# Mixing the last layer's result with the old state by one VectorE instruction instead of a diagonal matmul

## The chip, the core and the metric

One core of a Trainium2 chip runs the whole program once. The metric is the device time of that one execution in microseconds (us); the number given for a kernel is the median of several runs.

## What is computed

A graph with 6,250 nodes of 256 features and 100,000 edges passes two layers. The last part of the second layer is the one that matters here. For each node the messages of six relations have been summed; they are averaged, multiplied by a weight matrix of the node's type, mixed with the old state, normalized over the 256 features, and added to the residual:

```python
present = cnt.reshape(n, r) > 0
nrel = jnp.maximum(present.sum(-1), 1).astype(x.dtype)
t = (t_rel * present[..., None].astype(x.dtype)).sum(1) / nrel[:, None]
trans = typed_linear(t, Wa, ba)
alpha = jax.nn.sigmoid(skip)[node_type][:, None]
out = trans * alpha + x * (1.0 - alpha)
mu = out.mean(-1, keepdims=True)
var = out.var(-1, keepdims=True)
normed = (out - mu) * jax.lax.rsqrt(var + LN_EPS) * ln_g[node_type] + ln_b[node_type]
has_msg = present.any(-1)[:, None]
return jnp.where(has_msg, normed, x)          # the caller adds this to its own x
```

## The kernel before, in words

The program is a row of stages; the last one, `nodes_out`, works on 51 batches of 128 nodes, all nodes of a batch having one type. It is a software pipeline written out by hand. Each engine runs its own list of small functions, and `run_stages` gives each function a lag: in step s an engine runs, in the order of its list, the function with lag L for batch s - L. The loop body is unrolled four times, and semaphores join the engines.

The way of one batch: SyncE loads the node numbers (`load_in`). GpSimd gathers the relation sums of the 128 nodes from memory (`gather`, L1932, tile `acc_in`, lag 0). VectorE counts the relations that have messages (`counts`, L2044, lag 1), makes one factor for each relation and head (`at_least_one`, `masses`, `inverses`), and multiplies the whole gathered tile by them (`means`, L2074, 128 x 1536 elements, lag 1). TensorE transposes this (`turn`, L2160, lag 2) and ScalarE copies it out of PSUM (`mean_out`). TensorE multiplies by the relations' matrices (`relate`, L2170, lag 3), ScalarE copies again (`sum_out`), and TensorE runs `project` (lag 4). That one sums into `trans_p` in PSUM: two recorded matmuls with `keep_diag`, a diagonal matrix that holds 1 - alpha, and the old state `h1` (L2182); one matmul for the bias (L2184); four recorded ones for the weights, which hold alpha already (L2188). ScalarE makes `keep_diag` anew for each batch (`keep_part`, L1972). VectorE takes the statistics of `trans_p` (`stats` L2107, `variance` L2115, lag 4), ScalarE the root, VectorE the reciprocal and the shift (`scale` L2122, `shifts` L2127, lag 5), and ScalarE normalizes `trans_p` into `normed` (`norm`, L1998, lag 5). GpSimd multiplies by the type's gamma and adds its beta (`affine`, L1942 and L1947, lag 6). VectorE adds the rest (`finish`, L2139, tile `res`, lag 7; `other` was made by `others`, L2092, lag 3), and GpSimd scatters the batch to the output (`scatter`, L1957, lag 7).

Three orders matter. GpSimd's step is gather, scatter, affine. TensorE's is turn, project, relate. VectorE's is

```python
((1, counts), (7, finish), (1, at_least_one), (5, scale), (1, masses), (5, shifts), (1, inverses),
 (3, is_absent), (1, means), (4, stats), (3, others), (4, is_present), (4, variance))
```

so that `counts` of step s waits for the gather of batch s - 1, and all later functions of the step stand behind it. SyncE's step is load_in, load_x (lag 1), load_out (lag 5).

Of the kernel before, what the change touches and what calls it, by code (L numbers as in the profile page):

```python
# [24 lines left out]
ds = bass.ds  # L25
# [79 lines left out]
def wait_slot(eng, sems, item, dmas=1):  # L105

    eng.wait_ge(sems[item.slot(item.unroll)], item.round() * (16 * dmas))
# [1703 lines left out]
def nodes_out(nc, c):  # L1811
# [5 lines left out]
    with ExitStack() as ctx:  # L1817
        def sb(name, shape, dt=F32):
            return ctx.enter_context(nc.sbuf_tensor(name, shape, dt))
# [11 lines left out]
        x1, h1 = [t[:, 0:D] for t in x1h1], [t[:, D:2 * D] for t in x1h1]  # L1831
        type_f, keep_b = sb("type_of_f", [1, BATCHES]), sb("keep_of_batch", [P, BATCHES])
        of_kind = sb("batch_of_kind", [P, TYPES, BATCHES])
        keep_diag = [sb(f"keep_diag{k}", [P, P]) for k in range(2)]
        b_part = [sb(f"b_a_part{j}", [P, TYPES, D], BF16) for j in range(PARTS)]
        b_rest = sb("b_a_rest", [P, TYPES, D])
        b_rows, one_rows = sb("b_a_rows", [P, TYPES, D], BF16), sb("one_rows", [P, P], BF16)
# [33 lines left out]
        scaled_ready, biased_ready, res_ready = sem("scaled_o"), sem("biased_o"), sem("res_o")  # L1871
        stored, held = sems("out_stored", UN), sem("out_held")
        rows_filled, keep_ready, bias_ready = sem("b_a_rows_zero"), sem("keep_h_ready"), sem("b_a_parts")
        types_spread, kinds_ready, diag_ready = sem("types_spread"), sem("kinds_ready"), sem("keep_diag_ready")
        LANE, ROWS = 32, 96
        READY = 2 + PARTS
        acc_rows = c["acc_d"][0:NP * RELS, :].rearrange("(n r) f -> n (r f)", r=RELS)[0:N, :]
# [14 lines left out]
        with nc.Block() as block:  # L1892
            @block.sync
            def _(sp):
                def load_in(it):
                    k = it.slot(UN)
                    rows = ds(it.index * P, P)
                    rounds(sp, gathered, it)
                    sp.sem_inc(held, 1)
                    sp.dma_start(who_in[k][:], c["who_d"][rows, :]).then_inc(who_in_loaded[k], 16)  # L1900

                def load_x(it):
                    k = it.slot(UN)
                    rows = ds(it.index * P, P)
                    wait(sp, other_ready, it, UN)
                    sp.sem_inc(held, 1)
                    wait(sp, trans_summed, it, UN)
                    sp.sem_inc(held, 1)
                    sp.dma_start(x1h1[k][:], c["x1h1_d"][rows, :]).then_inc(x_loaded[k], 16)

                def load_out(it):
                    k = it.slot(UN)
                    rows = ds(it.index * P, P)
                    rounds(sp, stored, it)
                    sp.sem_inc(held, 1)
                    sp.dma_start(who_out[k][:], c["who_d"][rows, :]).then_inc(who_out_loaded[k], 16)

                run_stages(sp, BATCHES, ((0, load_in), (1, load_x), (5, load_out)), UN)
                for k in range(UN):
                    sp.wait_ge(stored[k], 16 * len(range(k, BATCHES, UN)))  # L1920
# [42 lines left out]
            @block.scalar  # L1963
            def _(act):
                act.activation(gain[:], skip[:], ACT.Sigmoid).then_inc(gain_ready, 1)

                def keep_part(it):
                    k = it.slot(2)
                    if isinstance(it.i, int) and it.index == 0:
                        act.wait_ge(w_ready, READY)  # L1970
                    wait(act, trans_summed, it, 2)
                    act.activation(keep_diag[k][:], c["ident"][:], ACT.Copy,  # L1972
                                   scale=keep_b[:, ds(it.index, 1)]).then_inc(diag_ready, 1)

                def mean_out(it):
                    k = it.slot(2)
                    wait(act, tT_summed, it, 2)
                    for pair in range(PAIRS):
                        act.wait_ge(meanT_turned, it.count(1, PAIRS, pair + 1))
                        act.copy(meanT[k][:, 2 * pair:2 * pair + 2], meanT_p[pair][:]).then_inc(meanT_ready, 1)  # L1980

                def sum_out(it):
                    k = it.slot(2)
                    wait(act, tT_summed, it)
                    wait(act, trans_summed, it, 2)
                    act.copy(tT[k][:], tT_p[:]).then_inc(tT_ready, 1)

                def root(it):
                    k = it.slot(UN)
                    wait(act, var_ready, it)  # L1990
                    wait(act, shift_ready, it, UN)
                    act.activation(std[k][:], mv[k][:, 1:2], ACT.Sqrt, bias=c["eps"][:]).then_inc(std_ready, 1)

                def norm(it):
                    k = it.slot(UN)
                    wait(act, shift_ready, it)
                    wait(act, res_ready, it, UN)
                    act.activation(normed[k][:], trans_p[it.slot(2)][:, 0:D], ACT.Identity, bias=shift[k][:],  # L1998
                                   scale=rstd[k][:]).then_inc(normed_ready, 1)

                run_stages(act, BATCHES, ((2, mean_out), (5, norm), (3, keep_part), (3, sum_out), (4, root)), UN)

            @block.vector
            def _(dve):
# [94 lines left out]
                    wait(dve, res_ready, it, UN)  # L2099
                    dve.tensor_scalar(present[k][:], count[k][:], 0.5, None, ALU.is_gt).then_inc(present_ready, 1)  # L2100

                def stats(it):
                    k = it.slot(UN)
                    wait(dve, trans_summed, it)
                    dve.sem_inc(held, 1)
                    wait(dve, var_ready, it, UN)
                    dve.bn_stats(stat[k][:], trans_p[it.slot(2)][:, 0:D]).then_inc(stat_ready, 1)  # L2107

                def variance(it):
                    k = it.slot(UN)  # L2110
# [19 lines left out]
                def finish(it):  # L2130
# [8 lines left out]
                    dve.scalar_tensor_tensor(res[k][:], normed[k][:], present[k][:], other[k][:], ALU.mult,  # L2139
                                             ALU.add).then_inc(res_ready, 1)  # L2140

                run_stages(dve, BATCHES, ((1, counts), (7, finish), (1, at_least_one), (5, scale), (1, masses),
                                          (5, shifts), (1, inverses), (3, is_absent), (1, means), (4, stats),
                                          (3, others), (4, is_present), (4, variance)), UN)

            @block.tensor
            def _(pe):
                kind = pe.alloc_register("kind_pe")
                pe.wait_ge(rows_filled, 2)
                pe.matmul(trans_p[0][:, 0:BATCHES], ones_f[:], type_f[:], start=True, stop=True).then_inc(types_spread, 1)  # L2150

                def turn(it):
                    k = it.slot(2)
                    wait(pe, mean_ready, it)
                    for pair in range(PAIRS):
                        if not (isinstance(it.i, int) and it.index == 0):
                            pe.wait_ge(meanT_ready, it.count(2, PAIRS, pair + 1))
                        for j in range(2):
                            for a in range(HALF):
                                ins = pe.transpose(meanT_p[pair][:, j, a, :], mean[k][:, 2 * pair + j, a * P:(a + 1) * P],  # L2160
                                                   c["ident"][:])
                        ins.then_inc(meanT_turned, 1)

                def relate(it):
                    k = it.slot(2)
                    wait(pe, meanT_ready, it, per=PAIRS)
                    wait(pe, tT_ready, it, 1)
                    for a in range(HALF):
                        for r in range(RELS):
                            ins = pe.matmul(tT_p[:, a, :], m_rel[:, r, a, :], meanT[k][:, r, a, :],  # L2170
                                            start=r == 0, stop=r == RELS - 1)
                    ins.then_inc(tT_summed, 1)

                def project(it):
                    k = it.slot(2)
                    t = type_of(pe, kind, it)
                    if isinstance(it.i, int) and it.index == 0:
                        pe.wait_ge(w_ready, READY)
                    wait(pe, normed_ready, it, 2)
                    wait_slot(pe, x_loaded, it)  # L2180
                    wait(pe, diag_ready, it)
                    pe.matmul(trans_p[k][:, 0:D], keep_diag[k][:], h1[it.slot(UN)],  # L2182
                              start=True, stop=False)
                    pe.matmul(trans_p[k][:, 0:D], one_rows[0:ROWS, :],  # L2184
                              b_rows[0:ROWS, ds(t, 1), :].rearrange("p o n -> p (o n)"), start=False, stop=False)
                    wait(pe, tT_ready, it)
                    for a in range(HALF):
                        ins = pe.matmul(trans_p[k][:, 0:D], tT[k][:, a, :],  # L2188
                                        w_a[:, ds(t * HALF + a, 1), :].rearrange("p o n -> p (o n)"),
                                        start=False, stop=a == HALF - 1)  # L2190
                    ins.then_inc(trans_summed, 1)

                run_stages(pe, BATCHES, ((2, turn), (4, project), (3, relate)), UN)


# [89 lines left out]
```

## Time and profile before

| | us |
|---|---|
| median of 3 runs | 3666.56 |
| lowest and highest | 3665.77, 3671.32 |
| the profiled execution | 3659.42 |
| its span in the trace | 3657.6 |
| start of `nodes_out` in the trace | 3329.3 |
| TensorE busy over the span | 3381.2 (92%) |
| VectorE busy over the span | 3185.6 (87%) |
| GpSimd busy over the span | 2390.0 (65%) |

The profile is of one execution. The times in its rows are counted from the start of the span. The stage that the change touches is the last 328 us.

### The profile page before, as it was taken

What the parts mean: (1) busy time and instruction counts of PE and PEld (TensorE: products, weight loads), DVE (VectorE), ACT (ScalarE), POOL (GpSimd) and SP (SyncE); (2) the same over time, 40 slices, a digit from 0 to 9 for tenths busy, and PEclk for the clock granted to TensorE, in tenths of its full rate; (3) what the DMA queues carried; (4) which work ended last, traced back from release to release, by engine and by line L of the source; (5) the groups of instructions that cost most, each with busy time, mean ns of one, the idle gap of its engine ahead of it and who ended that gap; (6) DMA issues with size and microseconds to landing.
All of it is one profiled execution on the core that took longest, in us unless ns stands there. A gap on an engine that the chain in (4) does not pass through costs nothing. (4 is left out here: it accounts for less than half of the span.)

```text
span 3657.6 us, 111781 instructions
## 1 busy us (share of the span) xinstructions
PE 3381.2 (92%) x25829; PEld 2771.8 (76%) x25830; DVE 3185.6 (87%) x9898; ACT 2594.7 (71%) x7607; POOL 2390.0 (65%) x2549
## 2 busy tenths in 40 slices
PE   3979999999999997996999999999999999997997
PEld 2547777777777775775888888888888888886996
DVE  6768999999999995664999999999999999996775
ACT  1856777777777774543878888888888888884553
POOL 3756777777777763554666666666666666663775
PEclk8989999999999997998999999999999999998998
DMA  3979999999999984776888888888888888884663
GB/s 102 263 230 309 301 296 301 298 298 298 299 298 300 300 253 165 276 258 224 254 235 239 240 236 239 237 239 237 238 238 239 238 237 239 236 237 150 213 208 126
DMA packets 604966, 898.40 MB, mean 246 GB/s; under 512 B 208971, under 2 KB 418646, under 8 KB 604371
## 3 DMA queue, kind: packets, MB, share of 16 engines
q0 software_dynamic: 164240, 566.71, 50.5%
q1 hardware_dynamic: 440643, 330.78, 30.2%
q8 instruction: 28, 0.46, 0.1%
q14 instruction: 55, 0.45, 0.0%
HBM read 724.25 MB, written 175.28 MB: 246 GB/s over the span
## 5 line engine op out<-in xcount | busy, mean ns | idle before, releaser
L1595 POOL DMA_INDIRECT kv1c<-kv_table,rec x900 | 865.9, 962 | 299.0 <-issue 284.6
L916 POOL DMA_INDIRECT kv<-kv_table,rec x832 | 848.3, 1020 | 282.3 <-issue 258.2
L1700 DVE CUSTOM_DVE_ANT_0 masked_scores<-score_p,far 126x384 f32<-126x384 f32 x1200 | 595.6, 551 | 30.2 <-issue 14.1
L1640 ACT ACTIVATE wv<-kv1c,wv 128x64 f32<-128x64 f32 x2400 | 605.9, 335 | 17.7
L954 ACT ACTIVATE gates<-gates_p 128x512 f32<-128x512 f32 x832 | 448.3, 591 | 77.5 <-PE gates_p L1087 77.5
L1803 PE MATMUL sum_p<-wv,hot 128*126 128x260 f32 x1800 | 477.7, 402 | 1.4 <-ACT wv L1640 1.4
L1759 PE MATMUL qe_p<-qrel,hotT 126*128 126x256 f32 x1800 | 443.0, 382 | 22.7 <-ACT hotT L1625 18.1
L1107 PE MATMUL sum_p<-msg,hot_weighted 128*124 128x256 f32 x1664 | 416.2, 393 | 5.3 <-ACT hot_weighted L962 5.3
L1759 PEld LDWEIGHTS qe_p<-qrel,hotT 126*128 126x128 f32 x1800 | 343.7, 191 | 74.9 <-ACT hotT L1625 18.7
L1107 PEld LDWEIGHTS sum_p<-msg,hot_weighted 128*124 128x124 f32 x1664 | 295.2, 187 | 116.2 <-issue 73.9
L1803 PEld LDWEIGHTS sum_p<-wv,hot 128*126 128x126 f32 x1800 | 316.1, 189 | 76.1 <-ACT wv L1640 1.8
L1605 POOL TENSOR_TENSOR faded<-acc,fade 126x260 f32<-126x260 f32 x300 | 186.2, 621 | 265.2 <-ACT fade L1648 255.2
L1680 DVE TENSOR_TENSOR qk<-qe_p,kv1c 128x768 f32<-128x768 f32 x300 | 285.7, 952 | 79.8 <-issue 47.7
L1783 PE MATMUL score_p<-scoreT,spread_head 32*126 32x128 f32 x7200 | 347.9, 282 | 0.8 <-ACT scoreT L1654 0.8
L1026 DVE CUSTOM_DVE_ANT_0 qe_p<-qe_p,gates 128x256 f32<-128x256 f32 x832 | 326.1, 452 | 0.0
L1792 PEld LDWEIGHTS peak_p<-peak,hotT 126*128 126x128 f32 x1800 | 223.4, 191 | 107.2 <-DVE peak L1708 71.0
L1792 PE MATMUL peak_p<-peak,hotT 126*128 126x4 f32 x1800 | 249.0, 256 | 52.1 <-DVE peak L1708 46.3
L1783 PEld LDWEIGHTS score_p<-scoreT,spread_head 32*126 32x126 f32 x7200 | 290.4, 184 | 6.4 <-ACT scoreT L1654 1.3
L1686 DVE TENSOR_REDUCE score_lanes<-qk 128x12 f32<-128x768 f32 x300 | 285.8, 953 | 4.8
L1011 DVE TENSOR_TENSOR qe_p<-qe_p,kv 128x1024 f32<-128x1024 f32 x208 | 254.8, 1225 | 12.2 <-DMA kv<-kv_table,rec 10.2
L1096 PEld LDWEIGHTS qe_p<-q_blk,hotT 124*128 124x128 f32 x1664 | 210.8, 189 | 71.6 <-issue 63.2
L962 ACT ACTIVATE hot_weighted<-hot,weight 128x124 f32<-128x124 bf16 x832 | 263.1, 388 | 0.2 <-DVE weight L1043 0.2
(285 smaller groups left out, 7392.0 us busy)
## 6 DMA issues: line engine op xcount, KB each, us to landing
key<-segment_keys SPq DMA_DIRECT2D x300, 192.0 KB
q_blk<-q_table SPq DMA_DIRECT2D x208, 256.5 KB
acc_table<-acc SPq DMA_DIRECT2D x300, 130.0 KB
qrel<-q_by_relation SPq DMA_DIRECT2D x300, 128.0 KB
feat<-in_edge_feat_t SPq DMA_DIRECT2D x208, 128.0 KB
agg_and_x_plus_h<-total SPq DMA_DIRECT2D x208, 128.0 KB
kv1c<-kv_table,rec POOLq DMA_INDIRECT x900
kv<-kv_table,rec POOLq DMA_INDIRECT x832
```

What stands on the lines that cost most here:

```text
L916: pool.indirect_dma_start(kv[it.slot(AHEAD)][:, t, :], None, c["kv0_d"], bass.IndirectOffsetOnAxis(ap=rec[k][:, t, 0:1].bitcast(I32), axis ...
L954: act.activation(gates[k][:, t, :], gates_p[t][:], ACT.Silu).then_inc(gates_ready, 1)
L1026: ins = dve.tensor_tensor_reduce(qe_p[:, t, :], qe_p[:, t, :], gates[k][:, t, 0:D], 1.0, 0.0, ALU.mult, ALU.add, attn[k][:, t:t + 1])
L1107: ins = pe.matmul(sum_p[:, k, :], hot_w[k][:, t, :], msg[k][:, t, :], start=t == 0, stop=t == T0 - 1)
L1595: pool.indirect_dma_start(kv[k][:, t, :], None, c["kv1_d"], bass.IndirectOffsetOnAxis(ap=rec[k][:, t, 0:1].bitcast(I32), axis=0)).then_inc ...
L1640: ins = act.activation(wv[k][:, t, h, 0:DK], kv[s][:, t, D + h * DK:D + (h + 1) * DK], ACT.Copy, scale=wv[k][:, t, h, DK:DK + 1])
L1686: dve.tensor_reduce(score[it.slot(U1)], qk[it.slot(2)][:], AX, ALU.add).then_inc(score_ready, 1)
L1700: dve.tensor_tensor_reduce(junk[k][:, h], score_p[:, :, h, :], far[it.slot(U1)][:], 1.0, FLOOR, ALU.subtract, ALU.max, top[s][:, h:h + 1]) ...
L1759: ins = pe.matmul(qe_p[:, t, :], hotT[k][:, t, :], qrel[s][0:SEG], start=True, stop=True)
L1783: ins = pe.matmul(score_p[:, t, h, :], spread_head[rows, h, :], scoreT[k][rows, :], start=True, stop=True)
L1792: ins = pe.matmul(peak_p[:, t, :], hotT[k][:, t, :], peak[it.slot(U1)][:], start=True, stop=True)
L1803: ins = pe.matmul(sum_p[:], hot[s][:, t, :], wv[k][:, t].rearrange("p h e -> p (h e)"), start=t == 0, stop=t == T1 - 1)
```

## The change

ScalarE's `keep_part` and TensorE's two recorded matmuls with `keep_diag` go. A new VectorE function `mix` (lag 4) reads the projection from PSUM, the old state `h1` and the factor of the batch, and writes the mixed state to a new tile `trans` in SBUF (four buffers). `stats` and `norm` read `trans`; TensorE's `project` waits for the `mix` of two batches before, where it waited for `norm`; SyncE's `load_x` waits for `mix`, where it waited for the projection. VectorE's list gets a new order: `others`, `mix` and `stats` now stand ahead of `means`.

```diff
-        keep_diag = [sb(f"keep_diag{k}", [P, P]) for k in range(2)]
+        trans = [sb(f"trans{k}", [P, D]) for k in range(UN)]
...
-                    wait(sp, trans_summed, it, UN)
+                    wait(sp, mixed_ready, it, UN)
...
-                def keep_part(it):
-                    k = it.slot(2)
-                    if isinstance(it.i, int) and it.index == 0:
-                        act.wait_ge(w_ready, READY)
-                    wait(act, trans_summed, it, 2)
-                    act.activation(keep_diag[k][:], c["ident"][:], ACT.Copy,
-                                   scale=keep_b[:, ds(it.index, 1)]).then_inc(diag_ready, 1)
-
...
-                    act.activation(normed[k][:], trans_p[it.slot(2)][:, 0:D], ACT.Identity, bias=shift[k][:],
+                    act.activation(normed[k][:], trans[k][:], ACT.Identity, bias=shift[k][:],
                                    scale=rstd[k][:]).then_inc(normed_ready, 1)
 
-                run_stages(act, BATCHES, ((2, mean_out), (5, norm), (3, keep_part), (3, sum_out), (4, root)), UN)
+                run_stages(act, BATCHES, ((2, mean_out), (5, norm), (3, sum_out), (4, root)), UN)
...
+                def mix(it):
+                    k = it.slot(UN)
+                    wait(dve, trans_summed, it)
+                    dve.sem_inc(held, 1)
+                    wait(dve, normed_ready, it, UN)
+                    dve.sem_inc(held, 1)
+                    wait_slot(dve, x_loaded, it)
+                    dve.scalar_tensor_tensor(trans[k][:], h1[k], keep_b[:, ds(it.index, 1)],
+                                             trans_p[it.slot(2)][:, 0:D], ALU.mult, ALU.add).then_inc(mixed_ready, 1)
+
                 def stats(it):
                     k = it.slot(UN)
-                    wait(dve, trans_summed, it)
+                    wait(dve, mixed_ready, it)
                     dve.sem_inc(held, 1)
                     wait(dve, var_ready, it, UN)
-                    dve.bn_stats(stat[k][:], trans_p[it.slot(2)][:, 0:D]).then_inc(stat_ready, 1)
+                    dve.bn_stats(stat[k][:], trans[k][:]).then_inc(stat_ready, 1)
...
-                run_stages(dve, BATCHES, ((1, counts), (7, finish), (1, at_least_one), (5, scale), (1, masses),
-                                          (5, shifts), (1, inverses), (3, is_absent), (1, means), (4, stats),
-                                          (3, others), (4, is_present), (4, variance)), UN)
+                run_stages(dve, BATCHES, ((1, counts), (7, finish), (1, at_least_one), (5, scale), (3, others),
+                                          (1, masses), (5, shifts), (4, mix), (1, inverses), (4, stats),
+                                          (1, means), (2, is_absent), (4, variance), (4, is_present)), UN)
...
-                    wait(pe, normed_ready, it, 2)
-                    wait_slot(pe, x_loaded, it)
-                    wait(pe, diag_ready, it)
-                    pe.matmul(trans_p[k][:, 0:D], keep_diag[k][:], h1[it.slot(UN)],
-                              start=True, stop=False)
+                    wait(pe, mixed_ready, it, 2)
                     pe.matmul(trans_p[k][:, 0:D], one_rows[0:ROWS, :],
-                              b_rows[0:ROWS, ds(t, 1), :].rearrange("p o n -> p (o n)"), start=False, stop=False)
+                              b_rows[0:ROWS, ds(t, 1), :].rearrange("p o n -> p (o n)"), start=True, stop=False)
```

## Rows read from the trace of the kernel before

**Rows 1.** Busy time by stretch: the steady part (stretch, us, each engine, clock, DMA, GB/s)

```profile
3380.00:3610.00 230.00, 223.89 (x1755) 210.40 (x1753) 169.78 (x568) 120.82 (x286) 167.79 (x162) 1.00 0.67 211
```

**Rows 2.** Chain that ended last, 3490 to 3540 us: two links of it

```profile
3497.72 5.15 DMA acc_in<-acc_table,who_in_o
...
3509.08 5.28 DMA acc_in<-acc_table,who_in_o
```

**Rows 3.** Instructions of L1932: ns min/median/max, first and last start

```profile
L1932 POOL DMA_INDIRECT acc_in<-acc_table,who_in_o x41: 988/994/1190, 3384.7 to 3612.1; - x41
```

**Rows 4.** Timeline of one step, VectorE and GpSimd (start us, duration us, instruction)

```profile
3502.90 0.99 POOL L1932 DMA_INDIRECT acc_in<-acc_table,who_in_o  x1 [0.15 <-issue]
...
3503.51 0.48 DVE L2139 SCALAR_TENSOR_TENSOR res<-normed,present,other 128x256 f32<-128x256 f32 x1 [0.32 <-issue]
3503.91 0.14 DVE L2052 TENSOR_SCALAR count_or_one<-count 128x1 f32<-128x1 f32 x1
3503.98 0.15 DVE L2122 RECIPROCAL rstd_o<-std_o 128x1 f32<-128x1 f32 x1
...
3504.60 0.30 DVE L2067 RECIPROCAL inv<-mass_o 128x24 f32<-128x24 f32 x1
...
3505.08 1.02 POOL L1957 DMA_INDIRECT out<-res,who_out_o  x1 [1.18 <-issue]
3505.12 1.76 DVE L2074 TENSOR_TENSOR mean<-acc_in,inv 128x1536 f32<-128x1536 f32 x1 [0.21 <-DVE inv L2067]
...
3506.11 1.35 POOL L1942 TENSOR_TENSOR normed<-normed,typed 128x256 f32<-128x256 f32 x1
3506.79 0.43 DVE L2107 BATCH_NORM_STATS2 stat_o<-trans_p 128x6 f32<-128x256 f32 x1
...
3507.13 0.61 DVE L2092 SCALAR_TENSOR_TENSOR other<-x1h_o,absent 128x256 f32<-128x256 f32 x1
...
3507.71 0.73 POOL L1947 TENSOR_TENSOR normed<-normed,typed 128x256 f32<-128x256 f32 x1 [0.26 <-POOL normed L1942]
...
3509.08 0.99 POOL L1932 DMA_INDIRECT acc_in<-acc_table,who_in_o  x1 [0.64 <-issue]
```

**Rows 5.** Timeline of TensorE in the same step

```profile
3501.53 1.47 PE L2160 MATMUL meanT_p<-ident,mean 128*128 128x128 f32 x12
3502.84 0.60 PE L2182 MATMUL trans_p<-x1h_o,keep_diag 128*128 128x256 f32 x2
...
3503.38 1.03 PE L2188 MATMUL trans_p<-w_a,tT 128*128 x4
...
3507.24 1.53 PE L2160 MATMUL meanT_p<-ident,mean 128*128 128x128 f32 x12 [0.15 <-issue]
```

**Rows 6.** Timeline at the start of the stage, GpSimd

```profile
3369.29 1.02 POOL L1957 DMA_INDIRECT out<-res,who_out_o  x1 [1.85 <-issue]
3370.33 2.31 POOL L1942 TENSOR_TENSOR normed<-normed,typed 128x256 f32<-128x256 f32 x1
```

**Rows 7.** Timeline at the start of the stage, VectorE

```profile
3369.99 2.07 DVE L2074 TENSOR_TENSOR mean<-acc_in,inv 128x1536 f32<-128x1536 f32 x1
```

**Rows 8.** Timeline at the end of the stage, when no gather and no mean is left

```profile
3625.55 0.75 POOL L1942 TENSOR_TENSOR normed<-normed,typed 128x256 f32<-128x256 f32 x1
3626.55 0.73 POOL L1947 TENSOR_TENSOR normed<-normed,typed 128x256 f32<-128x256 f32 x1 [0.26 <-POOL normed L1942]
...
3627.65 0.48 DVE L2139 SCALAR_TENSOR_TENSOR res<-normed,present,other 128x256 f32<-128x256 f32 x1 [2.38 <-POOL normed L1947]
```

**Rows 9.** Groups of VectorE instructions (busy us, mean ns), another stage, third operand in PSUM

```profile
L1036 DVE SCALAR_TENSOR_TENSOR total<-total,keep,sum_p 124x256 f32<-124x256 f32 x208 | 97.8, 470 | 7.0 <-PE sum_p L1107 6.1 <-issue 0.8
```

**Rows 10.** DMA issues, 3400 to 3600 us (KB, median us to landing)

```profile
who_in_o<-nodes_by_type SPq DMA_DIRECT2D x35, 1.0 KB, 3.5
```

**Rows 11.** Busy time by stretch in another stage, around a pause of TensorE

```profile
1446.00:1448.00 2.00, 0.00 (x0) 0.00 (x0) 0.78 (x2) 0.00 (x0) 1.70 (x2) 0.97 0.80 244
1448.00:1450.00 2.00, 1.47 (x7) 1.47 (x8) 0.00 (x0) 0.38 (x1) 1.39 (x3) 0.50 0.92 373
```

More of the change, by code:

```diff
@@ L1873, in nodes_out @@
         rows_filled, keep_ready, bias_ready = sem("b_a_rows_zero"), sem("keep_h_ready"), sem("b_a_parts")
-        types_spread, kinds_ready, diag_ready = sem("types_spread"), sem("kinds_ready"), sem("keep_diag_ready")
+        types_spread, kinds_ready, mixed_ready = sem("types_spread"), sem("kinds_ready"), sem("mixed_o")
         LANE, ROWS = 32, 96
@@ L2100, in is_present @@
                     dve.tensor_scalar(present[k][:], count[k][:], 0.5, None, ALU.is_gt).then_inc(present_ready, 1)
-                def stats(it):
+                def mix(it):
                     k = it.slot(UN)
@@ L2105, in stats @@
                     dve.sem_inc(held, 1)
+                    wait(dve, normed_ready, it, UN)
[3 more added lines that the diff above has]
+                                             trans_p[it.slot(2)][:, 0:D], ALU.mult, ALU.add).then_inc(mixed_ready, 1)
+                def stats(it):
+                    k = it.slot(UN)
+                    wait(dve, mixed_ready, it)
+                    dve.sem_inc(held, 1)
                     wait(dve, var_ready, it, UN)
-                    dve.bn_stats(stat[k][:], trans_p[it.slot(2)][:, 0:D]).then_inc(stat_ready, 1)
+                    dve.bn_stats(stat[k][:], trans[k][:]).then_inc(stat_ready, 1)
                 def variance(it):
```

## The prediction, made before the changed kernel was run

> **What bounds the kernel now.** I read the busy time by stretch first, for the last stage alone. In its steady part TensorE is busy 223.9 of 230 us at full granted clock, VectorE 169.8, GpSimd 167.8 [rows 1]. That looks like a TensorE bound, so the next view is the chain that ended last: it goes, again and again, through the landing of the gather, and not through TensorE. Two gathers on this chain start at 3497.72 and 3509.08, 11.36 us apart [rows 2], and between them lies one more gather [rows 4]: a ring that takes two steps, 5.68 us a step. Over 41 gathers a step takes (3612.1 - 3384.7) / 40 = 5.685 us [rows 3].
>
> The timeline of one step gives the rings. I call the start of `finish` f (3503.51).
>
> The gather ring: f to scatter start 1.57, scatter to L1942 1.03, L1942 start to L1947 start 1.60, L1947 0.73, then 0.15 to 0.64 to the next gather [rows 4], 5.15 to its landing [rows 2]. From the landing (3502.87) to f is 0.64. With a gap of 0.2 that sums to 10.92 for two steps; the trace has 11.36, so some 0.45 of gaps (the loop's back edge among them) is on top.
>
> The GpSimd ring, one step: the same first 4.93 us, and then 0.37 from L1947's end to the next `finish` (3627.28 to 3627.65, [rows 8]): 5.30.
>
> TensorE: from one `turn` to the next is 5.71, of which 3507.24 less the end of the work before it is some 0.26 of pause: work of 5.45 [rows 5].
>
> So three limits lie within 0.4 us, and the gather ring is the longest. One thing in it is not work of its own: L1942 takes 0.75 us at the end of the stage [rows 8] and 1.35 us here [rows 4]. It starts at 3506.11 while `means` runs (3505.12 to 3506.88) and ends at 3507.46, 0.58 after it. At the start of the stage it takes 2.31 us, beginning 0.34 after a `means` that ends at 3372.06, and ends at 3372.64, again 0.58 after [rows 6, 7]. GpSimd's multiply stands still while VectorE's long multiply runs.
>
> **The change, part by part.** There are 51 - 7 = 44 steps in which every function has a batch; I count with these.
>
> TensorE loses L2182, 0.43 us of a step (3503.27 less 3502.84, [rows 5]; the next matmul started there). ScalarE loses the making of `keep_diag`. Neither is on the gather ring: priced at nothing while that ring, or a longer one, covers them. If TensorE were the limit they would be worth up to 44 x 0.43 = 19 us.
>
> VectorE gains `mix`. This stage shows none; the nearest row is the same operation with its third operand in PSUM, 0.47 us [rows 9], against 0.48 and 0.61 for the two all-SBUF ones here [rows 4]. I take 0.47; bounds 0.4 and 0.61. VectorE is busy 74% of the time [rows 1], so 0.47 a step fits in 5.685 (0.74 x 5.685 + 0.47 = 4.7).
>
> The waits moved: `mix` waits for the projection, with `inverses`, `stats` and `means` queued behind it. That closes a ring of one step that was not there: `mix` to `stats` 0.62 (its time and a semaphore's 0.15), `stats` to `means` 0.34, `means` 1.76, to `turn` 0.1 to 0.36, `turn` to the end of the projection 3504.41 - 3501.53 - 0.43 = 2.45, and 0.15 back to `mix` [rows 4, 5, 9]. Sum 5.4 to 5.7. It is no longer than today's step, so this wait alone costs nothing, or little. SyncE's `load_x` now waits for `mix`, at most some 1.5 us later than the projection, with `load_out` and `load_in` queued behind it. The node numbers land 3.5 us after issue [rows 10] and the load issued in one step feeds a gather more than a step later: hidden.
>
> The order moved, and this is the part that costs. Today `means` starts 1.61 us after f [rows 4]. In the new order there lie ahead of it `finish` 0.40 (start to next start), `at_least_one` 0.07, `scale` 0.07, `others` 0.40, `masses` 0.16, `shifts` 0.07, `mix` with its latency 0.62, `stats` 0.34 (`inverses` is hidden in the latency): 2.13 us if everything is dispatched back to back, up to about 2.5 if the tiny ones take 0.2 each, as they do when they wait for one another. Meanwhile GpSimd reaches L1942 at f + 2.60, as now. So now its multiply starts as `means` has just begun, not when it is nearly over.
>
> What L1942 then takes: `means` from f + 2.13 to 2.5, for 1.76, then 0.58 to L1942's end, 0.26, L1947 0.73, and 0.37 to the next `finish`. That makes a step of 5.83 to 6.2. The one row that has the new alignment shows more: `means` that started 0.70 after a scatter took 2.07 instead of 1.76, that is, until 1.76 after the scatter's end [rows 6, 7]. By it `means` ends at f + 4.35 and the step is 4.35 + 0.58 + 0.26 + 0.73 + 0.37 = 6.29. If instead GpSimd gets in first (should `means` be dispatched after f + 2.60), L1942 runs to f + 3.35, `means` then to 5.11, L1947 stands behind it to 5.69, and the step is 6.06. The gather ring also grows, by the later end of L1947: with 5.83 in place of 4.93 it is 12.26 for two steps, 6.13 a step, and it does not take over. I take 6.2, between these and nearer the row that has the alignment. In the sum: 44 x (6.2 - 5.685) = 22.7 us. On the profiled execution (3659.42) that gives 3682.1; the median of the runs lies 7.1 higher, and on it the sum gives 3689.2.
>
> The Trainium skill has a rule here ("SBUF — State Buffer", section "SBUF: two separate sides"): VectorE and GpSimd share one pair of ports, and whichever instruction starts first keeps it for its whole length while the other fully blocks, if the VectorE instruction has two SBUF inputs and the GpSimd one reads SBUF. The trace agrees on the blocking. By the page's lock alone the whole 0.75 of L1942 would still follow the release, with the page's figure of about 115 ns, where the rows show 0.58; by the page's way the step would be some 0.28 longer and the time an estimated 12 us higher. The rows decide. The same page ("Who interferes with whom") infers that such a multiply does not contend with descriptor generation; by this the scatter would not hold `means`, and the step would be the 5.83 to 6.2 above; rows 6 and 7 speak against it.
>
> **The rivals.**
>
> *The blocking is as today or milder, and the new ring decides* (no change). If `means` slides but its start does not meet L1942, for instance since later steps shift the phase, the limit is the gather ring of 5.685 or the new ring of 5.4 to 5.7: -12 to +1 us, likeliest 3666. For it: GpSimd has pauses in each step (busy 73%, [rows 1]). Against it: no phase works. For `means` to start after L1947 it must start at f + 4.34, and VectorE then reaches the next `finish` only at about f + 6.8.
>
> *TensorE was the true limit* (faster). The place is TensorE's queue; it is 97% busy, and 0.43 of 5.45 goes. The step would fall to the new ring, 5.44 at best: 44 x 0.245 = 10.8 us less, 3655.8. It decides if the later `means` adds less than about 0.1 us to the gather ring. Against it: the gather ring explains the step to the last 0.01 us.
>
> *Two waits add up* (slower still). The late `means` delays `turn`, the projection, and so `mix`, which delays `means` again; with the hold of 0.31 the new ring is 5.7 to 6.0, and `others`, now 0.6 us after f, may meet the next gather. A step of 6.5 to 6.7: 44 x 0.9 = 40 us more, 3706. TensorE's clock is no large part of it: in another stage the granted clock fell to half only after some 3 us in which TensorE did nothing [rows 11], and the pause here would be about 6.2 - 5.02 = 1.2 us.
>
> **How the numbers follow.** L1942 or L1947 stuck behind the later `means`: 0.70, with an own range of 5.9 to 6.35 us a step, 3676 to 3696. Two waits add up: 0.08, 3706. The new ring or the old one decides: 0.16, 3655 to 3671, most of it near 3666. TensorE the limit: 0.06, 3656. Less than 0.2% (7.3 us) is about what a measurement of this kernel cannot tell from no change. The case without change spills a little to both sides, and the low end of the main case hardly reaches into it: faster 0.07, same 0.15, slower 0.78. For the range I leave out the fast case and half of the worst one: 3663 to 3702.
>
> **What would show it.** In the changed kernel's trace: a step of about 6.2 us by the starts of the gathers; L1942 (or its twin of the `affine` function) with a median of about 2.0 us where it had 1.35, or, if GpSimd gets in first, 0.75 for the first and 1.6 to 1.8 for the second multiply; `means` starting 2.1 to 2.5 us after `finish`, in part over 1.9 us long; TensorE busy some 81% of the steady part, at full clock; `mix` at 0.47 us and seldom waiting for TensorE; the chain going through `finish`, the scatter and `affine`, with few gather landings. The prediction is wrong if GpSimd's two multiplies are both about as long as before, if `means` starts less than 2 us after `finish`, or if `finish` does not wait for L1947.

## The result and the profile after

The changed kernel is slower. Over nine runs each its median is 3679.44 us (3670.03 to 3681.25) against 3669.23 us (3665.77 to 3672.43), 10.2 us more; the ratio of the runs is 1.0022, 95% interval [1.0012, 1.0033]. The forecast was 3689.2 us, 22.7 us more than the median of the three runs known then (3666.56). The profiled execution took 3672.24 us with a span of 3670.5.

The start of the last stage wanders from execution to execution, with stages before it that the change does not touch: its first gather lies between 3327.5 and 3356.1 us in the traces of this study. So beside the time of the runs I use two lengths from the traces: the stretch from the first gather of the stage to the end of the span (before: 3657.6 - 3333.2 = 324.4 us; after: 3670.5 - 3334.1 = 336.4, 12.0 more), and the step.

The gather's instructions after, in the steady part (ns min/median/max, first and last start), answer to [rows 3]; under them GpSimd's two multiplies and `means`:

```profile
L1932 POOL DMA_INDIRECT acc_in<-acc_table,who_in_o x40: 990/995/1004, 3392.9 to 3624.5; - x40
...
L1942 POOL TENSOR_TENSOR normed<-normed,typed x40: 752/762/775, 3389.8 to 3621.4; 128x256 f32<-128x256 f32 x40
...
L1947 POOL TENSOR_TENSOR normed<-normed,typed x40: 1942/1954/1957, 3390.8 to 3622.4; 128x256 f32<-128x256 f32 x40
...
L2066 DVE TENSOR_TENSOR mean<-acc_in,inv x40: 1773/1960/2076, 3390.2 to 3621.7; 128x1536 f32<-128x1536 f32 x40
```

A step takes (3624.5 - 3392.9) / 39 = 5.94 us where it took 5.685; 44 steps make 11.1 us. The first multiply of GpSimd is short now (0.76), the second is 1.95 in every step, where the kernel before had 1.35 and 0.73 [rows 4]. `means` is longer (median 1.96) than the 1.76 that it took.

Busy time of the steady part after, to set beside [rows 1]:

```profile
3380.00:3610.00 230.00, 200.67 (x1589) 189.00 (x1590) 177.84 (x585) 108.88 (x234) 183.27 (x156) 1.00 0.62 200
```

TensorE fell to 87% at the same full clock, and GpSimd rose. The timeline of one step after shows both rings (L2141 is now `finish`, L2084 `others`, L2101 `mix`, L2109 `stats`, L2066 `means`, L2186 the weights' matmuls, L2162 `turn`):

```profile
3506.06 0.48 DVE L2141 SCALAR_TENSOR_TENSOR res<-normed,present,other 128x256 f32<-128x256 f32 x1 [0.56 <-POOL normed L1947]
...
3506.71 1.03 PE L2186 MATMUL trans_p<-w_a,tT 128*128 x4
...
3507.56 1.02 POOL L1957 DMA_INDIRECT out<-res,who_out_o  x1 [0.72 <-issue]
...
3508.11 0.48 DVE L2101 SCALAR_TENSOR_TENSOR trans<-x1h_o,keep_of_batch,trans_p 128x256 f32<-128x256 f32 x1 [0.72 <-ACT normed L1990]
...
3508.57 0.77 POOL L1942 TENSOR_TENSOR normed<-normed,typed 128x256 f32<-128x256 f32 x1
3508.74 0.43 DVE L2109 BATCH_NORM_STATS2 stat_o<-trans 128x6 f32<-128x256 f32 x1
...
3509.08 1.89 DVE L2066 TENSOR_TENSOR mean<-acc_in,inv 128x1536 f32<-128x1536 f32 x1
...
3509.61 1.95 POOL L1947 TENSOR_TENSOR normed<-normed,typed 128x256 f32<-128x256 f32 x1 [0.26 <-POOL normed L1942]
...
3511.10 1.53 PE L2162 MATMUL meanT_p<-ident,mean 128*128 128x128 f32 x12 [0.68 <-DVE mean L2066]
...
3511.70 0.99 POOL L1932 DMA_INDIRECT acc_in<-acc_table,who_in_o  x1
3512.00 0.48 DVE L2141 SCALAR_TENSOR_TENSOR res<-normed,present,other 128x256 f32<-128x256 f32 x1 [0.64 <-POOL normed L1947]
```

GpSimd ring: `finish` to scatter 1.50, to L1942 1.01, to the end of `means` 2.40, to L1947's end 0.59, to the next `finish` 0.44: 5.94. Such a sum comes to the step by itself, whichever events are taken; what makes it a ring is that no link has slack. In the steps from 3396 to 3604 us `finish` starts 0.36 to 0.46 us after L1947's end and the scatter 1.01 to 1.10 us after `finish` ends, every time, while in after_inv_psum below, where this ring is not the limit, `finish` starts 1.14 to 1.75 us after L1947's end. `means` is dispatched at 3509.08 while L1942 runs, and its row ends at 3510.97, 1.63 after L1942's end: it is held. L1947 ends 0.59 after `means`, as the blocked multiply did before [rows 4, 6, 7]. (The row of `mix` names ScalarE as its releaser, but `mix` waits for the `norm` of four batches before, long done. In mix_waits below one `mix` starts at 3504.91, while the `norm` of that step, which started at 3504.80 and takes 0.60, still runs. What `mix` waited for is the projection.)

### The profile page after: what moved, and what is told of

Its sections match the earlier page's. It is cut to its first block and busy times, and to the rows that moved or that the text cites. A ratio compares the mean times of both kernels' runs of the same rounds, so it can differ in the third digit from the quotient of the medians.

```text
span 3670.5 us, 111627 instructions
## 1 busy us (share of the span) xinstructions
PE 3364.4 (92%) x25727; PEld 2759.6 (75%) x25728; DVE 3202.9 (87%) x9949; ACT 2584.7 (70%) x7556; POOL 2414.6 (66%) x2549
```

## The experiments

All times are ratios to the kernel before on the same chip, with the 95% interval. "Stretch" is the first gather to the end of the span, "step" the mean distance of the gathers in the steady part, both from the run's trace.

| kernel | ratio | interval | step | stretch |
|---|---|---|---|---|
| before | 1 | | 5.685 | 324.4 |
| changed | 1.0022 | 1.0012 to 1.0033 | 5.94 | 336.4 |
| mix_only | 0.9994 | 0.9982 to 1.0006 | 5.63 | 320.5 |
| order_only | 1.0033 | 1.0020 to 1.0046 | 5.94 | 336.1 |
| mix_waits | 1.0026 | 1.0017 to 1.0035 | 5.94 | 335.8 |
| no_diag_matmul | 1.0008 | 0.9998 to 1.0018 | 5.79 | 324.8 |
| after_inv_psum | 0.9994 | 0.9983 to 1.0004 | 5.74 | 326.5 |
| after_waits_inv | 0.9963 | 0.9950 to 0.9976 | 5.50 | 313.9 |
| waits_inv_again | 0.9977 | 0.9964 to 0.9991 | 5.48 | 313.8 |
| before_inv_psum | 0.9966 | 0.9950 to 0.9981 | 5.38 | 310.6 |
| mix_inv_psum | 1.0021 | 1.0009 to 1.0034 | 6.03 | 337.7 |
| mix_inv_loads | 1.0032 | 1.0021 to 1.0043 | 5.97 | 337.0 |
| after_loads | 1.0038 | 1.0026 to 1.0049 | 5.98 | 339.5 |
| late_mix | 1.0046 | 1.0029 to 1.0064 | 6.02 | 338.5 |
| late_mix_deep | 0.9979 | 0.9968 to 0.9989 | 5.74 | 322.5 |
| late_mix_lags | 0.9952 | 0.9935 to 0.9969 | 5.25 | 308.8 |
| late_mix_lags_2 | 0.9918 | 0.9901 to 0.9936 | 5.09 | 296.7 |

### The two halves of the change

mix_only keeps the mix on VectorE and puts `means` back ahead of it; order_only keeps the diagonal matmul and takes the new order.

```diff
 # mix_only, from the changed kernel
+ ((1, counts), (7, finish), (1, at_least_one), (5, scale), (1, masses), (5, shifts), (1, inverses),
+  (3, is_absent), (1, means), (4, mix), (3, others), (4, stats), (4, is_present), (4, variance))
 # order_only, from the kernel before
+ ((1, counts), (7, finish), (1, at_least_one), (5, scale), (3, others), (1, masses), (5, shifts),
+  (1, inverses), (4, stats), (1, means), (2, is_absent), (4, variance), (4, is_present))
```

> The mix is on VectorE as in the change, but means keeps its old place ahead of mix, others and stats. Theory A (the new order puts means into GpSimd's two multiplies, and that sets the step): means starts again about 1.6 us after finish, L1942 about 1.35 us, L1947 0.73, step 5.65 to 5.75, time within 5 us of the kernel before. Theory B (the mix itself is the cost: 0.48 us more on VectorE, wherever it stands): step 5.9, 10 us over before.

> The kernel before (diagonal matmul kept, no mix) with VectorE's new order: others and stats ahead of means. Theory A: the order alone makes the loss, one of the two GpSimd multiplies takes 1.9 us or more, step 5.8 to 6.1, time 6 to 16 us over before. Theory B (the mix is the cost): as before, within 3 us. Theory C (the cost is the ring of means, turn, projection and the VectorE instruction that waits for it): with the diagonal matmul the projection ends 0.43 us later, but 0.6 us of mix are gone, so step about 5.7 to 5.9.

The mix alone costs nothing: step 5.63, L1942 and L1947 as before. Its groups of GpSimd's multiplies (count, busy us, mean ns):

```profile
L1942 POOL TENSOR_TENSOR normed<-normed,typed 128x256 f32<-128x256 f32 x40 | 56.5, 1411 | 0.1
...
L1947 POOL TENSOR_TENSOR normed<-normed,typed 128x256 f32<-128x256 f32 x40 | 29.1, 726 | 10.3 <-POOL normed L1942 10.3
```

The order alone makes the whole loss: step 5.94, to the hundredth that of the changed kernel, with a ratio of 1.0033 against 1.0022, whose intervals overlap. One step of order_only:

```profile
3504.73 0.48 DVE L2139 SCALAR_TENSOR_TENSOR res<-normed,present,other 128x256 f32<-128x256 f32 x1 [0.64 <-POOL normed L1947]
...
3506.30 1.02 POOL L1957 DMA_INDIRECT out<-res,who_out_o  x1 [0.87 <-issue]
...
3507.26 2.45 DVE L2074 TENSOR_TENSOR mean<-acc_in,inv 128x1536 f32<-128x1536 f32 x1
3507.32 0.76 POOL L1942 TENSOR_TENSOR normed<-normed,typed 128x256 f32<-128x256 f32 x1
3508.34 1.95 POOL L1947 TENSOR_TENSOR normed<-normed,typed 128x256 f32<-128x256 f32 x1 [0.26 <-POOL normed L1942]
```

`means` starts 2.53 us after `finish`, 0.5 sooner than in the changed kernel (3.02), and is held for 0.69 instead of 0.13. What holds it back to 2.53 is again the projection, for which `stats` waits here (0.47 us in its row). Its end lies 4.98 us after `finish`, against 4.91, and the mean step is the same. That is what a ring through GpSimd looks like: what reaches it earlier only waits longer.

### Which ring: the waits of `mix` turned round

```diff
-                    wait(dve, trans_summed, it)
+                    wait_slot(dve, x_loaded, it)
                     dve.sem_inc(held, 1)
                     wait(dve, normed_ready, it, UN)
                     dve.sem_inc(held, 1)
-                    wait_slot(dve, x_loaded, it)
+                    wait(dve, trans_summed, it)
```

> The changed kernel with the three waits of mix turned round: old ones first, the projection's last, so that mix starts some 0.2 us sooner after the projection. Theory C (the TensorE ring sets the step of 5.94): step falls by up to 0.2, to about 5.75, and the time by up to 9 us. Theory A (the GpSimd ring, with means held by L1942 and L1947 by means): mix starts earlier, means is held longer (2.1 us instead of 1.9), step stays 5.9, time within 2 us of the changed kernel.

Here `mix` starts 0.14 us after the projection's last matmul instead of 0.37, `means` starts 2.8 us after `finish` instead of 3.0 and takes 2.21 us instead of 1.96 (medians), and the step stays 5.94. The ring over TensorE is not the limit of the changed kernel.

### Was TensorE the limit before?

no_diag_matmul drops the two recorded matmuls with `keep_diag` from the kernel before, and so leaves the old state out of the mix; the bias's matmul then starts the sum.

```diff
-                    pe.matmul(trans_p[k][:, 0:D], keep_diag[k][:], h1[it.slot(UN)],
-                              start=True, stop=False)
```

> The kernel before without its two recorded matmuls with keep_diag; ScalarE still makes keep_diag. Left out: the old state's part of the mix. If TensorE was the limit of the kernel before: step 5.3 to 5.45, 10 to 17 us less. If the gather ring was (my reading): step 5.6 to 5.69, at most 3 us less.

No gain: the median is 1.9 us over that of before, with an interval that holds no change, the stretch is 0.4 us longer, and the step of this trace is even 0.1 longer, for which I have no reason. The work that the change takes off TensorE was worth nothing.

### The blocking itself

`inv`, the second input of `means`, moves to PSUM; nothing else changes. If two SBUF inputs are the condition, GpSimd is free.

```diff
-        inv = [sb(f"inv{k}", [P, RELS * HEADS]) for k in range(2)]
+        inv = [ps(f"inv{k}", [P, RELS * HEADS]) for k in range(2)]
```

> The changed kernel with the tile inv (24 factors a node) in PSUM instead of SBUF, so that means has only one SBUF input; nothing else is changed. Theory A (means and GpSimd's multiplies shut each other out when means has two SBUF inputs, and this sets the step): L1942 0.75, L1947 0.73 where it had 1.95, means 1.76; the GpSimd ring falls to about 4.7 us and the ring over TensorE is the longest: step about 5.7, some 9 us less than the changed kernel, about the kernel before. Theory D (GpSimd's multiply is slow beside any VectorE work, not because of the second SBUF input): L1947 stays at 1.95, step 5.94, the changed kernel's time.

> The same, and the waits of mix turned round as in mix_waits. With the GpSimd ring out of the way the TensorE ring should be the limit, and what did nothing before should now tell: mix 0.1 to 0.2 sooner after the projection, step 5.5 to 5.65, 3 to 8 us less than after_inv_psum. If the gather ring (5.4) or VectorE is the limit instead, the two take the same time.

> The kernel before with inv in PSUM. Theory A: L1942 0.75 instead of 1.36, the gather ring loses 0.6 in two steps, to about 5.4, and TensorE's 5.45 is then the limit: step 5.45 to 5.5, 8 to 10 us less than before. Theory D: L1942 and time as before.

GpSimd's multiplies in after_inv_psum, and below those of before_inv_psum:

```profile
L1942 POOL TENSOR_TENSOR normed<-normed,typed 128x256 f32<-128x256 f32 x40 | 30.7, 767 | 0.1
...
L1947 POOL TENSOR_TENSOR normed<-normed,typed 128x256 f32<-128x256 f32 x39 | 28.4, 729 | 10.1 <-POOL normed L1942 10.1
```

```profile
L1942 POOL TENSOR_TENSOR normed<-normed,typed 128x256 f32<-128x256 f32 x42 | 32.3, 770 | 0.2
...
L1947 POOL TENSOR_TENSOR normed<-normed,typed 128x256 f32<-128x256 f32 x42 | 30.5, 726 | 10.8 <-POOL normed L1942 10.8
```

Both are back at 0.77 and 0.73 beside a running `means`, which takes 1.74 to 1.75. This is the rule of the Trainium skill ("SBUF — State Buffer", section "Who interferes with whom") that a VectorE instruction with at most one SBUF input, outside its two-port modes, does not contend with GpSimd. These two traces agree. With the GpSimd ring out of the way the ring over TensorE is the limit of the changed kernel: 5.74, and now turning the waits of `mix` round does pay, 5.50 (the median fell by 13.7 us between the two, more than the 3 to 8 expected). The same edit did nothing while the other ring was longer. In before_inv_psum TensorE is busy all the time (its window of the steady part reads 230.00 of 230.00) and the step is 5.38; the time fell by 15.5 us where 8 to 10 were expected, so TensorE's work is no more than 5.38, and not the 5.45 that I had read. It also shows what bound the kernel before: the shorter L1942 gave 0.3 us a step, and less work for TensorE (no_diag_matmul) gave nothing.

### The old order with `inv` in PSUM, and SyncE's queue

mix_inv_psum joins mix_only, the turned waits and `inv` in PSUM. mix_inv_loads and after_loads move one entry of SyncE's list:

```diff
-                run_stages(sp, BATCHES, ((0, load_in), (1, load_x), (5, load_out)), UN)
+                run_stages(sp, BATCHES, ((0, load_in), (3, load_x), (5, load_out)), UN)
```

> The mix on VectorE, in the old order (mix right after means), waits turned round, and inv in PSUM. TensorE's work is 5.02, the gather ring 5.4, VectorE's own chain of starts about 5.5 with its waits. Step about 5.45, 8 to 12 us less than the kernel before. If VectorE's chain is worse than I read it: 5.6, 3 us less.

> mix_inv_psum with load_x at lag 3 instead of 1 in SyncE's list, so that load_in no longer stands behind a load_x that waits for mix. If the wait of the gather for the node numbers, by way of SyncE's queue, is what made mix_inv_psum's step 6.03: that wait goes, step 5.45 to 5.6, 5 to 10 us less than the kernel before. If something else did (VectorE's chain, TensorE's start after a late means): step stays above 5.8.

> The changed kernel with load_x at lag 3 in SyncE's list, nothing else. Theory A (GpSimd ring sets the step): step 5.94, within 3 us of the changed kernel, 8 to 11 over before. Theory E (SyncE's queue, in which load_x now waits for mix with load_in behind it, costs a part of the loss): step down to 5.8 or less, 5 us or more below the changed kernel.

mix_inv_psum missed: step 6.03, not 5.45. Its waits between 3400 and 3600 us (who waited for what: us in total, times, longest) have a line that neither the kernel before nor the changed one has:

```profile
POOL acc_in L1932 <- DMA who_in_o<-nodes_by_type: 18.7, 13, 1.8
```

The node numbers are late, by way of SyncE's queue, where `load_in` stands behind a `load_x` that waits for a `mix` at the end of VectorE's step. mix_inv_loads takes that line away and the step hardly falls: 5.97, a second miss. Its timeline shows another thing:

```profile
3508.32 0.72 POOL L1947 TENSOR_TENSOR normed<-normed,typed 128x256 f32<-128x256 f32 x1 [0.26 <-POOL normed L1942]
3508.39 0.94 DVE L2084 SCALAR_TENSOR_TENSOR other<-x1h_o,absent 128x256 f32<-128x256 f32 x1
```

`others` has two SBUF inputs too, and now it meets L1947 and is held, 0.94 instead of 0.48. VectorE's chain is full in this order, so it shows: between 3400 and 3600 us only one of its waits, of 0.9 us, is for anything but itself and its own issue. mix_only has the same order, a median of 0.56 for `others` and a step of 5.63; here they are 0.94 and 5.97. The 0.38 and the 0.34 fit, but no run separates them. For the changed kernel after_loads gives the answer: 5.98, no gain, so SyncE's queue is no part of the loss.

### Cutting the ring over TensorE

late_mix moves `mix`, `stats` and what follows one step later, with `inv` in PSUM and the turned waits; late_mix_deep also moves everything but `load_in` and `gather` one more. SyncE's `load_x` and `load_out` had lags 3 and 5 in late_mix, 4 and 6 in late_mix_deep, so that `load_out` stood one step nearer to the scatter than in the changed kernel. late_mix_lags and late_mix_lags_2 are the same two with SyncE's lags moved along: 2 and 6, 3 and 7.

```diff
+ ((1, counts), (8, finish), (1, at_least_one), (6, scale), (4, others), (1, masses), (6, shifts),
+  (5, mix), (1, inverses), (5, stats), (1, means), (2, is_absent), (5, variance), (4, is_present))   # VectorE
+ ((2, mean_out), (6, norm), (3, sum_out), (5, root))                                                # ScalarE
+ ((0, gather), (8, scatter), (7, affine))                                                           # GpSimd
+ ((0, load_in), (2, load_x), (6, load_out))                                                         # SyncE, late_mix_lags
```

> The new order, inv in PSUM, load_x at lag 3, and mix, stats and all after them one step later (mix at lag 5, finish at lag 8), so that mix never waits for the projection of its own step: the TensorE ring is cut. The gather ring (5.35 to 5.4) is then the limit. Step 5.35, one step more at the end (4.6 us): 44 x 0.33 - 5 = 10 us less than before, about as after_waits_inv. If the ring over TensorE was not the limit of after_waits_inv: step 5.5, 3 us less than before.

> late_mix with everything but load_in and gather one more step later, so that the gather ring spans three steps instead of two. Limits left: TensorE's work 5.02, VectorE's starts about 4.9 to 5.1, GpSimd 4.7. Step 5.05 to 5.2, two steps more at the end: 12 to 18 us less than before. If the gather ring was not the limit of late_mix: the step stays, and the time is 4 to 5 us over late_mix.

> late_mix with SyncE's lags moved along with the rest (load_x 2, load_out 6), so that load_out waits for the same distance of stores as in the changed kernel. If the ring through TensorE (means, turn, projection, mix) was what held after_waits_inv at 5.50, cutting it now gives 5.3 to 5.4, and with one step more at the end about the time of after_waits_inv, within 4 us. If late_mix was slow for another reason than SyncE's queue, the step stays at 5.9 to 6.0, 14 us or more over before.

> The same, with all but load_in and gather one step later still: the gather ring is spread over three steps. If the gather ring was the limit left: step 5.05 to 5.2, with two more steps at the end 12 to 18 us less than before. If VectorE or GpSimd are the limit: step 5.3 and 5 us less than before.

> after_waits_inv once more on this chip, to stand beside the two: step 5.50, 11 to 15 us less than before, if its first result holds from chip to chip; within 5 us of before if it was a matter of that chip.

late_mix missed (6.02) and late_mix_deep came half way (5.74): both show GpSimd waiting for node numbers, late_mix

```profile
POOL acc_in L1932 <- DMA who_in_o<-nodes_by_type: 23.9, 10, 2.9
```

for `load_in` stood behind a `load_out` that waited for a store of the step before. With SyncE's lags in order the step is 5.25, under 5.48 of waits_inv_again on the same chip, so the wait of `mix` for its own step's projection was the second limit, and in late_mix_lags_2, with the gather ring spread over three steps, it is 5.09, with TensorE busy for 219.2 of the 220 us from 3380 to 3600. Both beat the kernel before; late_mix_lags_2, at 0.9918, is the fastest kernel of this study.

In the last three kernels the steps came out about as expected, the times less so. waits_inv_again took 7.9 us less than before, where 11 to 15 were expected, with the step and the stretch of after_waits_inv. late_mix_lags_2 took 26.3 us less, where 12 to 18 were expected. Its stretch is 27.7 us shorter: 23.9 by the steps of 40 gathers, 12.6 by a shorter start of the stage, for which I have no reason, against 8.8 that the end is longer.

## Why the prediction was right in kind and wrong in size

Right: before the change the chain went through the gather and not through TensorE, and taking 0.43 us a step off TensorE is worth nothing (no_diag_matmul). `mix` costs 0.48 us, is hidden (mix_only), and was taken at 0.47. The loss comes from the order alone (order_only), through GpSimd's multiply that stands behind `means` (after_inv_psum takes the loss away). The new ring over TensorE lies just under the other: its links in the step shown are, from the end of `means`, 0.13 to `turn`, 2.50 to the end of the projection, 0.37 to `mix`, 0.63 to `stats`, 0.34 to `means` and 1.76 for `means` when nothing holds it, together 5.73, and 5.74 was measured once it was alone; I had 5.4 to 5.7.

Wrong: the size. The sum was 44 x (6.2 - 5.685) = 22.7 us; measured are 44 x (5.938 - 5.685) = 11.1 in the trace and 10.2 between the medians. The term mis-sized is the new step: 6.2 taken, 5.94 measured. The step of the prediction that failed is "`means` from f + 2.13 to 2.5", and with it the choice of "nearer the row that has the alignment". The sum of starts left out the wait for the projection in front of `mix`: 2.05 us after `finish` instead of 1.17 (and the signs had `mix` "seldom waiting for TensorE"). So `means` is dispatched at f + 3.02, after L1942 has begun (f + 2.51), and GpSimd gets in first. That was the prediction's own sub-case, priced at 6.06, or 16.5 us; the trace has 5.94, mostly since the hold of `means` ends 0.13 before L1942's row does. I had worked out the ring over TensorE, at up to 5.7, and used it only as a rival to the step, not for the phase of `means` within the step, where its wait decided who meets whom.

The alignment of [rows 6, 7] came about once in the steady part. In order_only `means` starts at f + 2.52 to 2.88 in the steps from 3396 to 3604 us, and L1942 has a median of 0.77: GpSimd nearly always wins. But in one step VectorE did:

```profile
3605.82 0.48 DVE L2139 SCALAR_TENSOR_TENSOR res<-normed,present,other 128x256 f32<-128x256 f32 x1 [0.56 <-POOL normed L1947]
...
3608.35 2.33 POOL L1942 TENSOR_TENSOR normed<-normed,typed 128x256 f32<-128x256 f32 x1
3608.36 1.74 DVE L2074 TENSOR_TENSOR mean<-acc_in,inv 128x1536 f32<-128x1536 f32 x1
...
3612.04 0.48 DVE L2139 SCALAR_TENSOR_TENSOR res<-normed,present,other 128x256 f32<-128x256 f32 x1 [1.14 <-POOL normed L1947]
```

That step took 6.22 us from `finish` to `finish`. So the price of this alignment was about right, and what failed is which of the two long instructions goes first.

Two readings of the prediction were weaker than they sounded. "The gather ring explains the step to the last 0.01 us" compares the step with itself, for the 11.36 us is the distance of two gathers; the links added up to 10.92. It was the runs that showed this ring to be the limit. And the 6.29 let the scatter hold `means`, by [rows 6, 7]; in [rows 4] `means` starts 0.04 us after the scatter and takes its usual 1.76. The scatter can hold it only in its later part, if at all; no run separates that from L1942, which follows at once.

The rival "two waits add up" fell: the hold of `means` fills the gap between the ring over TensorE (5.73) and the GpSimd ring (5.94) and adds nothing to the longer one; in mix_waits `means` came earlier, was held longer, and the step stayed. "TensorE was the true limit" fell with no_diag_matmul.

## What to carry to other kernels

In a hand-made pipeline, sum each ring of waits and divide by the steps it spans; then place each instruction within the step by all its waits, for the place decides which instructions of VectorE and GpSimd collide. A freed engine off the longest ring gives nothing, and a reordering that hides latencies on one engine can cost more by where it puts a long instruction. An edit on a ring just under the longest gives nothing until the longest is gone. Before reordering around a collision, take it away: one small operand moved to PSUM was worth more here than the whole change.

## What the runs showed of the hardware that I had not expected

- `means` with its row starting at 3507.26 lost against a GpSimd multiply whose row starts at 3507.32 (order_only), and took 2.45 us; at 3608.36 `means` won against a multiply whose row starts 0.01 us earlier. The start of a row does not say which of the two is held.
- The hold works against VectorE as well: `others`, 0.48 us alone, took 0.94 behind L1947 (mix_inv_loads).
- Two increments of a semaphore, and the two waits beside them that had long been met, cost 0.23 us between the decisive wait and the instruction: 0.37 us from the matmul's end to `mix` against 0.14 with that wait last.
- The fixed part of the time moves too: 28.6 us lie between the earliest and the latest first gather of the stage in these traces, after stages with the same code.
- GpSimd's gather is held by `means` too. At the start of the stage, in the kernel before and below it in before_inv_psum:

```profile
3348.03 1.76 DVE L2074 TENSOR_TENSOR mean<-acc_in,inv 128x1536 f32<-128x1536 f32 x1
3348.26 2.34 POOL L1932 DMA_INDIRECT acc_in<-acc_table,who_in_o  x1 [0.30 <-issue]
```

```profile
3350.17 1.75 DVE L2074 TENSOR_TENSOR mean<-acc_in,inv 128x1536 f32<-128x1536 f32 x1
3350.59 0.94 POOL L1932 DMA_INDIRECT acc_in<-acc_table,who_in_o  x1 [0.31 <-issue]
```

With `inv` in SBUF the gather ends 0.81 us after `means` (so it does in the changed kernel, 2.20 us long, and in mix_only, 2.14); with `inv` in PSUM it takes its usual 0.94 beside a running `means`.
